# Six tiles instead of eight under way when the attention units begin

## The reference

```
xn = layernorm(x)                                  # 4 x 1024 x 512
q  = rope(rmsnorm(xn @ Wq + bq));   16 heads of 128
w  = softmax over each 4 tokens of (xn @ Wcmp + bcmp)
entries = sum over each 4 tokens of w * xn         # 256 per batch
ck = rope(rmsnorm(entries @ Wk + bk));  cv = entries @ Wv + bv
sparse = softmax of the 8 largest causal q.ck  @ cv
lk, lv = rope(rmsnorm(xn @ Wlk + blk)), xn @ Wlv + blv
local  = softmax of q.lk over the own and the previous 128 tokens @ lv
out = x + (0.5 * (sparse + local)) @ Wo + bo + fp8(xn/2) @ fp8(W2/2) * 4
```

## Time and profile before

| | |
|---|---|
| median of three runs | 2489.04 us |
| the profiled execution, its own time | 2486.87 us |
| its span, first to last instruction | 2484.7 us |
| TensorE busy | 2452.7 us (99%) |
| VectorE busy | 2001.1 us (81%) |
| GpSimd busy | 1802.2 us (73%) |
| ScalarE busy | 1658.9 us (67%) |

### The profile page before, as it was taken

One profiled execution on the slowest core, in us unless ns is written; L12 is line 12 of the kernel. 1 busy time (PEld: TensorE's weight loads), 2 busy tenths in 40 slices (PEclk: granted clock), 3 DMA queues, 4 the chain that ended last, 5 costly groups with the idle time before them and its releaser, 6 DMA issues. The chain is left out here.

```text
span 2484.7 us, 55981 instructions
## 1 busy us (share of the span) xinstructions
PE 2452.7 (99%) x15446; PEld 2174.0 (87%) x15446; DVE 2001.1 (81%) x6637; ACT 1658.9 (67%) x4818; POOL 1802.2 (73%) x3214
## 2 busy tenths in 40 slices
PE   7999999999999999999999999999999999999998
PEld 6888888888888888888888888888888888888887
DVE  7788888888788878888778888887878878888886
ACT  5667676767676666666666666666666666666665
POOL 6787787776787767777768776677777767676674
PEclk9999999999999999999999999999999999999999
DMA  5433233333342232332442222333235213212301
GB/s 160 135 107 113 64 116 115 118 109 116 126 124 71 70 95 65 67 81 68 148 155 62 91 69 66 95 70 79 67 128 164 94 59 101 83 53 94 99 10 52
DMA packets 189674, 233.42 MB, mean 94 GB/s; under 512 B 23859, under 2 KB 107317, under 8 KB 189365
## 3 DMA queue, kind: packets, MB, share of 16 engines
q1 hardware_dynamic: 188788, 229.58, 31.1%
q10 hardware_dynamic: 576, 0.26, 0.0%
HBM read 163.70 MB, written 65.03 MB: 92 GB/s over the span
## 5 line engine op out<-in xcount | busy, mean ns | idle before, releaser
L1699 POOL TENSOR_TENSOR t<-raw,tB 128x128 f32<-128x128 f32 x512 | 225.5, 461 | 532.9 <-DVE raw L1243 532.8
L1052 ACT ACTIVATE ch<-bVC,blT 128x128 fp32r<-128x128 f32 x512 | 160.1, 364 | 542.8 <-PE bVC L790 542.6
L695 PE MATMUL bQK<-wh,xh 128*128 128x512 f32 x1024 | 424.3, 414 | 0.0
L696 PE MATMUL bQK<-wl,xh 128*128 128x512 f32 x1024 | 403.9, 394 | 0.0
L697 PE MATMUL bQK<-wh,xl 128*128 128x512 f32 x1024 | 401.3, 392 | 0.0
L1643 POOL TENSOR_TENSOR r<-ss,mh 128x4 f32<-128x4 f32 x256 | 287.6, 1124 | 58.7 <-DVE ss L1251 55.8
L711 PE MATMUL bVC<-wh,xh 128*128 128x256 f32 x1024 | 310.2, 303 | 0.0
L1279 DVE CUSTOM_DVE_ANT_0 P<-bS,cst 128x256 f32<-128x256 f32 (+1 forms) x512 | 204.1, 399 | 125.0 <-PE bS L743 119.6
L1019 ACT ACTIVATE P<-P,nm,r 128x256 f32<-128x256 f32 (+1 forms) x512 | 295.2, 583 | 0.0
L713 PE MATMUL bVC<-wh,xl 128*128 128x256 f32 x1024 | 289.4, 283 | 0.0
L712 PE MATMUL bVC<-wl,xh 128*128 128x256 f32 x1024 | 289.0, 282 | 0.0
(11 more groups left out here) (199 smaller groups left out, 7615.8 us busy)
## 6 DMA issues: line engine op xcount, KB each, us to landing
wh<-kept SPq DMA_DIRECT2D x144, 256.0 KB, 4.1
wl<-kept SPq DMA_DIRECT2D x144, 256.0 KB, 4.7
kept<-wh SPq DMA_DIRECT2D x48, 256.0 KB, 3.1
kept<-wl SPq DMA_DIRECT2D x48, 256.0 KB, 3.4
woh<-kepto SPq DMA_DIRECT2D x48, 256.0 KB, 3.4
wol<-kepto SPq DMA_DIRECT2D x48, 256.0 KB, 3.8
ini<-in_hidden_states SPq DMA_DIRECT2D x24, 256.0 KB, 3.5
xs<-xsh SPq DMA_DIRECT2D x24, 256.0 KB, 2.6
```

Of the source, the lines that this page charges most:

```text
L695: e.matmul(bQK[:, :], a, b, start=kt == 0, stop=False)
L696: e.matmul(bQK[:, :], a, bl, start=False, stop=False)
L1699: last = e.tensor_tensor(t2[:, :, :, d_], raw[:, u % 2, :, :, s_], tB[:, :, u % 8, d_].unsqueeze(1).broadcast_to([128, 2, 2, 32]), ALU.mult)
```

## The change

The prefix has six steps instead of eight. Tiles 0 to 3 are turned in it, tiles 4 to 7 in the steps 0 to 3, beside units. The logits of tiles 4 to 7 go to the bank bY instead of half of the bank of the scores. The entries of tiles 4 to 7 come one step earlier in the tile's life. The projection of the first block of compressed keys (`ckv`) comes in step 0 instead of step -1, its turn stays in step 1, and for steps below 8 the stages of blocks have other places inside a step: `ckv` behind the second half of the projection, `turn_ck` behind values and logits, `lo_ck` and `hi_ck` later, `weights4` at the head of VectorE's step, `power_ck` and `power_x` behind `power_qk`. Two fills of eight matmuls in step 1 go, two of three move by a step.

```diff
-AHEAD = 8
+AHEAD = 6
...
-"wm": (3, 3, 4, None), "et": (3, 4, 8, None),
+"wm": (3, 3, 4, None), "et": (3, 3, 8, None),
...
-BLOCK_LAGS = {"kv": (4, 5, 7, 12), ... "turn": (6, 6, 9, 14), ...
+BLOCK_LAGS = {"kv": (3, 3, 7, 12), ... "turn": (4, 4, 9, 14), ...
...
         def logits_of(t):
-            return (bY if t >= FIRST_TILES else bS[1])[:, 0:128]
+            return (bY if t >= 4 else bS[1])[:, 0:128]
...
             def logits(t):
                 e.wait_ge(S["dg"], t + 1)
-                if t >= FIRST_TILES:
+                if t >= 4:
                     e.wait_ge(S[free["Y"][0]], free["Y"][1])
                     free["Y"] = ("eg", t + 1)
...                                                      TensorE
-                if s in (-3, -2):
+                if s in (-2, -1):
                     fill(3)
             for s in range(NU):
-                if s == 1:
-                    fill(8)
+                k, early = block_at(s, "turn"), s < 8
                 if u0 is not None:
                     proj_qk(u0, 0)
-                if block_at(s, "turn") is not None:
-                    turn_ck(block_at(s, "turn"))
-                if s == 1:
-                    fill(8)
+                if k is not None and not early:
+                    turn_ck(k)
...
-                if block_at(s, "kv") is not None:
+                if block_at(s, "kv") is not None and not early:
                     ckv(block_at(s, "kv"))
...
                 if tile_at(s, "max") is not None:
                     logits(tile_at(s, "max"))
+                if k is not None and early:
+                    turn_ck(k)
                 if u0 is not None:
                     proj_qk(u0, 1)
+                if block_at(s, "kv") is not None and early:
+                    ckv(block_at(s, "kv"))
...                                                      VectorE
-                if block_at(s, "lo") is not None:
-                    lo_ck(block_at(s, "lo"))
+                if tile_at(s, "wm") is not None and early:
+                    weights4(tile_at(s, "wm"))
...
+                if k is not None and early:
+                    lo_ck(k)
                 if u0 is not None:
                     put_qk(u0)
...
-                if tile_at(s, "wm") is not None:
+                if tile_at(s, "wm") is not None and not early:
                     weights4(tile_at(s, "wm"))
+                if block_at(s, "put") is not None and early:
+                    lo_cv(block_at(s, "put"))
...                                                      GpSimd
-                if block_at(s, "rope") is not None:
+                if block_at(s, "rope") is not None and s >= 8:
                     power_ck(block_at(s, "rope"))
...
                 if u0 is not None:
                     power_qk(u0)
+                if s >= 0 and s < 8 and tile_at(s, "power") is not None:
+                    power_x(tile_at(s, "power"))
+                if block_at(s, "rope") is not None and s < 8:
+                    power_ck(block_at(s, "rope"))
```

More of the change, by code:

```diff
@@ L93 @@
 LAGS = {"stats": (0, 0, 0, 0), "power": (0, 0, 0, 0), "norm": (1, 1, 1, 1), "turn": (2, 2, 3, 3), "hi": (2, 2, 3, 3),
-        "lo": (2, 2, 3, 3), "max": (2, 2, 3, None), "ew": (3, 3, 4, None), "wm": (3, 3, 4, None), "et": (3, 4, 8, None),
+        "lo": (2, 2, 3, 3), "max": (2, 2, 3, None), "ew": (3, 3, 4, None), "wm": (3, 3, 4, None), "et": (3, 3, 8, None),
         "park": (None, None, 4, 4), "spread": (None, None, None, 2), "gather": (None, None, None, 3),
@@ L98 @@
         "fold": (None, None, None, 10)}
-BLOCK_LAGS = {"kv": (4, 5, 7, 12), "put": (4, 5, 7, 12), "rope": (4, 5, 7, 12), "turn": (6, 6, 9, 14), "hi": (6, 6, 9, 14),
-              "lo": (6, 6, 9, 14)}
+BLOCK_LAGS = {"kv": (3, 3, 7, 12), "put": (3, 3, 7, 12), "rope": (3, 3, 7, 12), "turn": (4, 4, 9, 14), "hi": (4, 4, 9, 14),
+              "lo": (4, 4, 9, 14)}
 def tile_at(s, stage):
@@ L729, in scores @@
                     if u == 0:
-                        e.wait_ge(S["eg"], FIRST_TILES)
+                        e.wait_ge(S["eg"], 4)
                     if b == 0 and i % 4 == 0:
@@ L1170, in run_scalar @@
                     exp_4(tile_at(s, "share"))
-                if block_at(s, "hi") is not None:
-                    hi_ck(block_at(s, "hi"))
+                k, early = block_at(s, "hi"), s < 8
+                if k is not None and not early:
+                    hi_ck(k)
                 if tile_at(s, "hi") is not None:
@@ L1175, in run_scalar @@
                     cast_x(tile_at(s, "hi"))
-                if block_at(s, "put") is not None:
+                if block_at(s, "put") is not None and not early:
                     put_kv(block_at(s, "put"))
@@ L1190, in run_scalar @@
                     squares(u0)
+                if block_at(s, "put") is not None and early:
+                    put_kv(block_at(s, "put"))
                 if u2 is not None:
@@ L1533, in run_vector @@
                 u0, u1, u2, u3, u4, u5 = (unit_at(s, lag) for lag in range(6))
-                if block_at(s, "lo") is not None:
-                    lo_ck(block_at(s, "lo"))
+                k, early = block_at(s, "lo"), s < 8
+                if k is not None and not early:
+                    lo_ck(k)
+                if tile_at(s, "wm") is not None and early:
+                    weights4(tile_at(s, "wm"))
                 if u2 is not None:
@@ L1826, in run_gpsimd @@
                     normalise_p(u2, 1)
-                if s >= 0 and tile_at(s, "power") is not None:
+                if s >= 8 and tile_at(s, "power") is not None:
                     power_x(tile_at(s, "power"))
```

## The result

| | before | after |
|---|---|---|
| median of six runs, same chip | 2487.78 us | 2504.17 us (2503.03 to 2504.67) |
| span of the profiled execution | 2484.7 us | 2501.3 us |
| TensorE busy | 2452.7 us | 2457.9 us |
| mean granted clock | 1.000 | 0.997 |

The changed kernel is slower: ratio 1.0066, 95% interval 1.0056 to 1.0076, which is 16.4 us (13.9 to 18.9). I had forecast 2494.5 us in a range of 2487 to 2501, counted from 2489.04 us, the median of three of these six runs of the kernel before. The sign was right, the size was not: three times the loss, and outside the range.

What follows compares the result with a forecast made beforehand. TensorE, without later slack, bounds the kernel, so start-up delay reaches the end. Early start keeps 0.9 to 2.5 us, steps 2 and 3 lose 7.1, steps 4 and 5 give 0: 2489.04 + 5.5 = 2494.5 us, range 2487 to 2501.

Steps and rivals of the forecast that it cites:

- T(6): Start of the second half of step 6's Q/K projection; the forecast gave no value for it.
- ring: Steps 1 to 3: dependent chain from half projection through rotation, normalising, entries to logits; 10.85 then 10.11 us, loss 7.1.
- T(3): Start of the second half of step 3's Q/K projection; forecast 66.2 to 67.8 us against 61.49 before.
- T(5): Start of the second half of step 5's Q/K projection; forecast 4 to 7 us after 80.32.
- rival 2: TensorE falls to its lower speed in the gaps of steps 1 to 3: 6.7 us more, 2501 us; chance 15%.
- The front: Prefix and steps 0 and 1: step 0 starts 8.6 us earlier, of which only 0.9 to 2.5 are left.
- T(1): Start of the second half of step 1's Q/K projection; forecast 45.2 to 46.8 us against 47.66 before.
- The add of unit 0: Add ending step 0's Q/K projection on VectorE; forecast to start at 36.2 to 37.8 us, against 41.68 before.
- Rival 1: Steps 1 to 3 stay short, each under about 7.5 us, so the early start is kept: some 2486.5 us; chance 20%.
- steps 4 and 5: Key turn's wait gone against entries and keys' projection added: between -0.7 and +1.1 us, taken as 0.
- The key turn's wait: TensorE's 1.75 us wait for the scaled keys at 77.94 should go, since the turn comes 2.3 us later.
- rival 3: Behind step 5: GpSimd's power delays the softmax and probabilities' transposes; another 3 us lost, 2497.5 us; chance 10%.

Runs made afterwards that it cites:

- logits' bank: Changed kernel with the logits of tiles 4 to 7 in a bank of their own, so they don't wait for the entries' copy; 2498.94 us, 1.0047.
- tile early: Changed kernel with VectorE and ScalarE doing the tile's work of steps 0 to 3 ahead of the unit's; 2499.63 us, 1.0047.
- all edits: Changed kernel with tile's work first, own banks for logits and second block's keys, and entries' weights right behind the rotation add; 2486.79 us, 1.0001.
- the tile early, the logits apart and the weights ahead: Changed kernel with tile's work before the unit's, logits in their own bank, next entries' weights ahead of the compressed keys' work; 2490.91 us, 1.0017.

## Why the prediction was right in sign and wrong in size

The difference at T(6), 15.5 us, splits into three by the kernel with fills in the gaps (filled), which has the clock at 1.00 from 40 us on and the same order:

| part | how it is read | us | predicted |
|---|---|---|---|
| ring of steps 0 to 3 | T(3) filled 66.76 less 61.49 before | +5.3 | +5.5 |
| steps 3 to 6 | 31.33 filled less 28.34 before | +3.0 | 0 up to T(5), nothing behind it |
| clock | T(6) 105.36 less 98.09 filled | +7.3 | 0 in the forecast; 6.7 as rival 2 |

**The front.** Right at both ends, in part by luck between them. The first half projection starts at 27.92 (forecast 28.3), T(1) is 45.94 (45.2 to 46.8). The add of unit 0 is at 35.67, half a us ahead of my range, which VectorE's timeline shows beside what follows it:

```profile
35.67 0.69 DVE L1249 TENSOR_TENSOR raw<-bQK,br 128x512 f32<-128x512 f32 x1 [1.09 <-PE bQK L697]
...
38.02 0.67 DVE L1262 TENSOR_TENSOR raw<-t 128x256 f32<-128x256 f32 x1 [0.28 <-POOL t L1715]
...
42.79 1.06 DVE L1433 TENSOR_SCALAR wm<-cst,smt 128x32 f32<-128x32 f32 x1
```

The gap of 2.35 us from the raw add to the rotation add is the 2.37 of the earlier trace rows. But from this add to T(1) are 10.27 us where I had summed 9.0, and 0.7 of the excess stand between the end of the scaled keys and the entries, where `wm` takes 1.06 us. Step 0 ended 1.3 us ahead of the middle of my range and step 1 took 1.3 more, so the two errors cancel in T(1). (The upper end of that range was also added wrongly: 34.5 + 3.1 is 37.6, not 37.8.) Of the 8.6 us of early start 1.7 are left at T(1), inside my 0.9 to 2.5.

**The ring.** Right in mechanism and size, at the full clock: 10.74 and 10.12 us, T(3) at 66.76 in my 66.2 to 67.8. Its links are each within some 0.3 us of mine, and their differences cancel. The two edits that take links out of it brought T(3) 2.4 us (logits' bank) and 5.4 us (tile early, 65.51) ahead of the changed kernel's. Rival 1, that the early start is kept, fell: it needed steps under 7.5 us.

**Steps 4 to 6.** Here a term was mis-sized, and another left out. I took 0 for steps 4 and 5, with bounds of -0.7 and +1.1, and the filled kernel shows +1.3 up to T(5) (20.16 us from T(3), 18.83 before). Another +1.7 come between T(5) and T(6) (11.17, 9.51 before), where my sum had already ended, since I had named the difference at T(5) the forecast. The key turn's wait did go, as I said. But I priced what the late turn removes and not what then stands behind it: the low part of the keys comes later, and since the turned keys lie in the bank bT, which the next transposes need, these wait 1.9 us. The keys' high copy is done at 93.28 us; ahead of the low part VectorE has the split of an output weight, 1.28 us, and then 2.0 us of the softmax and of the values of other units:

```profile
92.30 1.28 DVE L1353 TENSOR_TENSOR wol<-wr,woh 128x512 fp32r<-128x512 f32 x2
95.58 0.41 DVE L1509 TENSOR_TENSOR qkl<-bT,qkh 128x256 fp32r<-128x256 f32 x1
```

And in step 4 the entries of tile 7 wait 1.35 us for `wm`, which I had counted as work and not as a wait. Neither is rival 3, which named GpSimd's power and the probabilities: it is the same outcome (a backlog) by another queue.

**The clock.** This is the step of the forecast that failed, the term with which the time left the range: "Against it: after the wait of 1.75 us at 77.94 the next matmuls still ran at full speed". From one wait in a busy neighbourhood I concluded for steps with three waits each, gave the fall of the clock 15%, and made it an alternative to the ring, while it is a consequence: the ring leaves TensorE idle, and the idle time brings the clock down. With the ring at 55% or more, the fall belonged into the sum. My own price for it, 6.7 us, is near the 7.3 measured by luck: I had 2.7 us in each of two and a half steps up to T(3), and the changed kernel lost 4.1 there against the filled one (2.5, then 1.6) and 3.2 from T(3) to T(6), where I had nothing. The rival's 2501 us also lacks the 3.0 of steps 4 to 6. From the median of all six runs before, 2487.78 + 5.3 + 3.0 + 7.3 = 2503.4 us, where 2504.17 was measured; the profiled executions differ by 1.1 us behind T(6). The split is that of single traces, with the uncertainty of the marks; by the medians the clock is 7.5. The Trainium skill, "TensorE: Matmul & The Clock Gate", section "The HAM clock gate", says that the array falls to half its clock after idling. Section "HAM oscillation — how this bites in real kernels" of the same page of the Trainium skill describes a kernel that pays this again in each round of its loop, behind one wait for a DMA. The traces agree on the fall and on its return: it comes in steps 1, 2, 4 and 5 (0.70, 0.50, 0.61, 0.60). They differ in what stands ahead of it: several waits for other engines, of which none was over 2.6 us, and step 3 with such waits has no fall.

No version beat the kernel before: the best, with all edits, is level with it.

## What to carry to other kernels

When a change lets the busiest engine idle for several short waits in a row, give what its clock may do behind them a place in the sum: it was worth more than the waits' own ring here (7.3 us beside 5.3), and it shows in the stretches behind the waits, not in those that hold them. A test for it costs one kernel: put matmuls that nobody reads into the gaps; if the time falls, the clock was part of the loss. (In the kernel before, taking such matmuls out changed nothing, and the clock held.) And when work is moved later in its step to lose a wait, price what is queued behind the moved instruction and which bank it keeps: two waits of 0.9 and 0.8 us took the place of one of 1.8.

## What the runs showed of the hardware

- In the changed kernel the granted clock fell to 0.50 to 0.70 in stretches behind several waits of 0.5 to 2.6 us. It stayed at 1.00 behind waits of 1.0 and 0.9 us (fills removed) and behind the 1.75 us at 77.94; but it fell to 0.72 in the kernel with the weights earliest, where the waits from 37 to 43 us are 0.4, 0.5 and 0.7 us. Two waits had both outcomes: the 1.90 us for the second keys' low part (0.60 behind it in the changed kernel, 1.00 with the logits' own bank) and the 1.46 us of step 4's entries (0.59 and 1.00). So the length of a wait alone doesn't decide; what does stays open.
- In the first 30 us matmuls take nearly double time (entries 1.92 us, 1.08 later) while the table shows a granted clock of 1.00 from 20 us on, before and after the change. There the duration tells the speed and the clock's column doesn't; why is open.
- A VectorE instruction on 128x32, the weights `wm`, took 0.33 us at 78.02 and 1.06 at 42.79, on the ring of step 1. GpSimd's subtraction of 128x512 numbers ran from 42.55 to 43.81, and the small one ended at 43.85. At 30.33 it was the same, 1.14 us beside a product of 128x512 numbers:

```profile
42.55 1.26 POOL L1729 TENSOR_TENSOR wl<-wr,wh 128x512 fp32r<-128x512 f32 x1
...
30.17 1.26 POOL L1799 TENSOR_TENSOR tA<-tA,P 128x512 f32<-128x512 f32 x1
```

```profile
30.33 1.14 DVE L1433 TENSOR_SCALAR wm<-cst,smt 128x32 f32<-128x32 f32 x1
...
78.02 0.33 DVE L1433 TENSOR_SCALAR wm<-cst,smt 128x32 f32<-128x32 f32 x1
```

The changed kernel makes such weights eight times. Once no GpSimd instruction ran beside (21.76), and it took 0.30 us; the other seven took 0.33 to 1.14 us, and each ended 0.03 or 0.04 us behind the GpSimd instruction that was under way when it began. In the kernel with the tile early, the logits apart and the weights ahead, those of step 1 come at 39.15 beside a GpSimd power of 128x4 numbers, and take 0.30 us. So the kind of GpSimd instruction counts, and no run varied that alone. The Trainium skill, "SBUF — State Buffer", section "SBUF: two separate sides", says that VectorE and GpSimd share a pair of ports which, for some kinds of VectorE instruction, the one that starts first holds to its end; the ends, 0.04 us apart, agree with that.
